# A two-layer graph network on one core: where the edge product is computed and added

## The chip, the cores and the metric

One NeuronCore of one Trainium2 chip runs the whole program in one launch. The metric is the device time of that launch in microseconds. Engines are named as in the profile: PE (TensorE) with its weight loads PEld, DVE (VectorE), ACT (ScalarE), POOL (GpSimd), and SP, which only issues transfers here.

## The reference, cut to what matters

There are 12,500 nodes with 128 features and 200,000 edges, sorted by their target node. Two layers follow each other. The second one needs, for every edge, the product of its 128 edge features with a 128x128 matrix.

```python
h = relu(layernorm(x))
x = x + gin(h)                     # neigh = segment_sum(h[src], dst); two dense layers after it
h = layernorm(relu(layernorm(x))) * gamma + beta
t = gelu(concat([h[src], edge_attr], axis=1) @ Wt + bt)
  # = gelu( (h @ Wt[:128] + bt)[src]  +  edge_attr @ Wt[128:] )
attn = sum((t @ Wk + bk) * (h[dst] @ Wq + bq), -1) * edge_weight / sqrt(128)
a = softmax of attn over the edges of one target node
out = x + gelu(segment_sum(a * (t @ Wv + bv), dst))
```

The line after `t` shows the split that both kernels use. The source part is computed once for each node and kept in memory as `source_rows` (L130). The edge part, `edge_attr @ Wt[128:]`, is here called the edge product.

## The kernel before, in words

**Chunks.** The edges are cut into 98 chunks of 2,048 (`CHUNK`, L39): 16 columns of 128 edges, one edge to a partition. Four columns are a quad, so a chunk has four quads. Both sweeps go over all chunks. A loop around each sweep repeats it when the targets of a block of 256 edges span over 40 nodes; with these inputs each sweep runs once.

**First sweep** (`gin_sweeps`, L510). For chunk c, SP loads the source indices and the transposed edge features (L548, L550). POOL gathers 16 columns of source rows with one indirect transfer each (L506, called at L561), after a small tensor operation that stands in front of each chunk (`hold`, L500). TensorE computes the edge product of chunk c, one matmul of 128 edges with `wt` for each column (L572), into two PSUM banks. ScalarE copies each quad from PSUM to `ews` (L602) and issues its store to the DRAM tensor `edge_products` (L610). Then TensorE takes up the gathered rows of chunk c-1 and sums them into windows of 40 nodes by a matmul with a one-hot matrix (L583). VectorE builds the one-hot matrix (L467) and adds the eight windows of a chunk to `acc` (L629).

**Between the sweeps** `node_mid` runs the dense layers of all nodes and writes `source_rows`.

**Second sweep** (`attention_sweeps`, L858). Each engine has a step that handles four chunks at different ages: f (the newest), mid (one older), late (two older) and last (three older). The order within a step is written out by hand for every engine.
- SP (L936 to L967), for f: indices, then four quads of stored edge products, each after VectorE's addition of the same quad of the chunk before (L944), then edge weights, the queries `qw` and their bias `cw`; then for last the broadcast `fade` (L960).
- POOL (L971): waits for the indices and until the sums of chunk c-4 have used its buffer (there are four `t` buffers, L974); then 16 gathers, in groups of four with a semaphore each.
- VectorE (L1220): `add_products` (L1118) waits for each gathered quad and its edge product and adds the one to the other in SBUF (L1123); then `add_sums` of last (L1163), the mask `misses` of f (L1127), the maxima of mid (L1183, eight at L1200, then L1203, L1205, L1216), and the scores of f (L1129 to L1161).
- ScalarE (L1099): gelu of a quad in place in SBUF (L1079), then the copy of the turned quad from PSUM to `tT` (L1084); at the end of the step the exponentials of mid (L1090, L1093).
- TensorE (L1051): it turns each gelu quad with four transposes (L988) into one of two PSUM banks, and multiplies the turned quad with the queries (L1003). Between these stand the transposes of mid's scores (L1012), the row of maxima (L1021) and the spread of the running maximum (L1027). The step ends with the sums of late (L1035 to L1049): 16 matmuls of a gelu tile with the exponentials (L1040) and 16 with ones (L1047).

A float32 matmul appears in the trace as two instructions, a transpose as one. `node_end` closes with the last projection and gelu.

Of the kernel before, what the change touches and what calls it, by code (L numbers as in the profile page):

```python
# [121 lines left out]
def build_gnn(nc, a):  # L122

    with ExitStack() as ctx:
# [9 lines left out]
        ew = nc.dram_tensor("edge_products", [NCH, P, COLS * D], F32, kind="Internal").ap()  # L134
# [21 lines left out]
        gin_sweeps(nc, a, g, h0, ew, first, span)  # L156
        node_mid(nc, a, g, res, arow, qk, ck)
        with nc.sbuf_tensor("rows", [33, NW], F32) as rows:
            g["rows"] = rows
            attention_sweeps(nc, a, g, arow, ew, qk, ck, fades, first, span)  # L160
            node_end(nc, a, g, res)
# [348 lines left out]
def gin_sweeps(nc, a, g, h0, ew, first, span):  # L510


    with ExitStack() as ctx:
        st = Stage(nc, ctx, "gin")
        wt = st.sb("wt_edge", [P, D])
# [3 lines left out]
        evT, ews = st.two("evT", [P, COLS * P]), st.two("ews", [P, COLS, D])  # L519
        sums = [st.ps(f"sums{j}") for j in range(2)]  # L520
        ew_ps = [st.ps(f"ew_ps{j}") for j in range(2)]
# [4 lines left out]
        ev_in, ew_out = st.sem2("ev_in"), st.sem2("ew_out")  # L526
        hot_ready, sums_ready, added = st.sem("hot_ready"), st.sem("sums_ready"), st.sem("added")
        product, ew_sb = st.sem("product"), st.sem("ew_sb")
        src = a["src_chunks"]
        dve_regs = [nc.vector.alloc_register(f"gin_win{b}") for b in range(BPC)]  # L530
        with nc.Block() as block:
            @block.sync
            def _(sp):
                sp.dma_start(wt[:, :], a["Wt"][D:2 * D, :]).then_inc(setup, 16)
                sp.dma_start(g["start"][:, :], first).then_inc(setup, 16)
                sp.wait_ge(setup, 32)
        with nc.Fori(0, span + 1, WIN):
            st.clear(gathers=True)
            next_windows(nc, g, st, w, hs[0][:, :, :].rearrange("p k d -> p (k d)"))
            with nc.Block() as block:  # L540
                @block.sync
                def _(sp):
                    def step(f, bk):
                        if not f:
# [20 lines left out]
                def _(pe):  # L565
                    def edge_product(f, q):
                        if q == 0:
                            wait(pe, ev_in[f.j], 16 * (f.h + 1))
                        wait(pe, ew_sb, QUADS * f.c + q - 1)
                        for k in range(4):  # L570
                            at = (4 * q + k) * P
                            mm = pe.matmul(ew_ps[q % 2][:, k * P:(k + 1) * P], evT[f.j][:, at:at + P],  # L572
                                           wt[:, :], start=True, stop=True)
                        mm.then_inc(product, 1)

# [11 lines left out]
                    def step(f, bk):  # L587
                        if f:
                            for q in range(QUADS):
                                edge_product(f, q)  # L590
                        if bk:
                            add_rows(bk)
                    over_chunks(pe, step)

                @block.scalar
                def _(act):
                    def step(f, bk):
                        def copy_product(q):
                            wait(act, product, QUADS * f.c + q + 1)
                            if q == 0:  # L600
                                wait(act, ew_out[f.j], 16 * f.h)
                            act.activation(ews[f.j][:, 4 * q:4 * q + 4, :].rearrange("p k d -> p (k d)"),  # L602
                                           ew_ps[q % 2][:, :], ACT.Copy).then_inc(ew_sb, 1)

                        if not f:
                            return
                        for q in range(QUADS):
                            copy_product(q)
                        wait(act, ew_sb, QUADS * (f.c + 1))
                        act.dma_start(ew[bass.ds(f.c, 1)].rearrange("a p n -> p (a n)"),  # L610
                                      ews[f.j][:, :, :].rearrange("p k d -> p (k d)")).then_inc(ew_out[f.j], 16)
                    over_chunks(act, step)
                    for j in range(2):
                        act.wait_ge(ew_out[j], 16 * (NCH // 2))
# [243 lines left out]
def attention_sweeps(nc, a, g, arow, ew, qk, ck, fades, first, span):  # L858
# [4 lines left out]
    with ExitStack() as ctx:  # L863
# [5 lines left out]
        ews = [st.sb(f"ews{q}", [P, COLS // QUADS, D]) for q in range(QUADS)]  # L869
# [20 lines left out]
        ew_in = [st.sem(f"ew_in_{q}") for q in range(QUADS)]  # L890
        wgt_in = st.sem2("wgt_in")
        names = ("summed", "t_sb", "tT_ps", "tT_sb", "sc_q", "miss", "biased", "prod", "score", "attn", "masked", "xm", "xm_ps",
# [10 lines left out]
        with nc.Block() as block:  # L903
            @block.sync
            def _(sp):
                sp.dma_start(g["start"][:, :], first).then_inc(setup, 16)

# [3 lines left out]
                sp.wait_ge(setup, 48)  # L911
# [18 lines left out]
        with nc.Fori(0, span + 1, WIN):  # L930
            st.clear(gathers=True)
            next_windows(nc, g, st, w, t[0][:, :, :].rearrange("p k d -> p (k d)"))
            with nc.Block() as block:
                @block.sync
                def _(sp):
                    def loads(f):  # L936
# [6 lines left out]
                        for q in range(QUADS):  # L943
# [170 lines left out]
                def _(v):  # L1114
# [266 lines left out]
```

## Time and profile before

| | |
|---|---|
| median of 3 runs | 4691.19 us (4682.67 to 4695.08) |
| profiled execution, its own time | 4713.18 us |
| its span in the trace | 4711.2 us |
| mean granted clock of TensorE | 0.729 |
| busy PE / DVE / ACT / POOL | 65% / 40% / 28% / 67% |
| first gather of the first sweep to the last one's end | 139 to 2128 us |
| first gather of the second sweep to the last one's end | 2443 to 4526 us |

The profile takes one execution. Its rows name an instruction group by line, engine and operation, then what it writes and reads, how many there were, the busy time, the mean of one in ns, and the idle time in front of it with the releaser that ended it.

### The profile page before, as it was taken

How to read it: one execution, taken by the hardware profiler on the slowest of the kernel's cores; microseconds unless marked ns; L12 is line 12 of the kernel's file. 1: busy time of each engine (PE TensorE's matmuls, PEld its weight loads, DVE VectorE, ACT ScalarE, POOL GpSimd, SP SyncE). 2: the span in 40 equal slices, each digit the busy share in tenths (PEclk: the TensorE clock that was granted, in tenths of full speed). 3: DMA queues.
4: the chain of work that ended last, by engine and by line, in shares of the span. 5: the costliest groups of instructions: out<-in, count | busy, mean ns of one | idle time of the engine just before them, and what ended most of it. 6: DMA issues, size and time to landing. Idle time of an engine off the chain costs nothing. (4 is left out here: it accounts for less than half of the span.)

```text
span 4711.2 us, 72968 instructions
## 1 busy us (share of the span) xinstructions
PE 3054.1 (65%) x20056; PEld 2809.9 (60%) x20057; DVE 1865.5 (40%) x5996; ACT 1313.3 (28%) x2114; POOL 3162.9 (67%) x3343
## 2 busy tenths in 40 slices
PE   2466666556665666664746777676767777777774
PEld 1466566556665666663326767676666666766664
DVE  3111111111111111114545666666666666666643
ACT  4111111111111111113633343343333343434324
POOL 0677777777777777770037777777777777777730
PEclk9666666666666666667877787788888787888776
DMA  4455445555455545542334444444444444444423
GB/s 123 150 159 159 148 152 159 159 159 157 144 158 159 159 144 156 159 141 64 102 101 115 125 122 117 113 127 121 118 124 116 124 116 123 117 126 118 121 61 101
DMA packets 364892, 614.69 MB, mean 130 GB/s; under 512 B 109604, under 2 KB 237335, under 8 KB 339624
## 3 DMA queue, kind: packets, MB, share of 16 engines
q1 hardware_dynamic: 237284, 298.04, 22.2%
q0 software_dynamic: 100352, 205.72, 16.9%
q10 hardware_dynamic: 27076, 109.29, 5.6%
q14 instruction: 160, 1.31, 0.1%
q8 instruction: 20, 0.33, 0.0%
HBM read 477.54 MB, written 135.23 MB: 130 GB/s over the span
## 5 line engine op out<-in xcount | busy, mean ns | idle before, releaser
L506 POOL DMA_INDIRECT attention_t<-source_rows,attention_idx x1568 | 1587.9, 1013 | 463.4 <-issue 447.7
L506 POOL DMA_INDIRECT gin_hs<-h_rows,gin_idx x1568 | 1506.7, 961 | 463.1 <-issue 463.0
L583 PE MATMUL gin_sums<-gin_hot,gin_hs 128*128 128x40 f32 x3136 | 686.6, 413 | 763.7 <-DMA gin_hs<-h_rows,gin_idx 763.7
L583 PEld LDWEIGHTS gin_sums<-gin_hot,gin_hs 128*128 128x128 f32 x3136 | 672.5, 330 | 781.8 <-issue 725.0
L629 DVE TENSOR_TENSOR acc<-acc,gin_sums 128x40 f32 x784 | 154.5, 197 | 1760.7 <-PE gin_sums L583 1670.3
L602 ACT ACTIVATE gin_ews<-gin_ew_ps 128x512 f32<-128x512 f32 x392 | 234.1, 597 | 1768.3 <-PE gin_ew_ps L572 1768.0
L988 PE MATMUL attention_tT_ps<-ident,attention_t 128*128 128x128 f32 x1568 | 366.5, 378 | 385.4 <-ACT attention_t L1079 385.4
L572 PE MATMUL gin_ew_ps<-gin_wt_edge,gin_evT 128*128 128x128 f32 x3136 | 566.2, 363 | 7.6 <-DMA gin_evT<-in_edge_attr_cols 7.6
L572 PEld LDWEIGHTS gin_ew_ps<-gin_wt_edge,gin_evT 128*128 128x128 f32 x3136 | 554.1, 277 | 8.9 <-DMA gin_evT<-in_edge_attr_cols 8.8
L988 PEld LDWEIGHTS attention_tT_ps<-ident,attention_t 128*128 128x128 f32 x1568 | 266.9, 199 | 421.8 <-issue 367.1
L1003 PE MATMUL attention_sc_q<-attention_qw,attention_tT 128*128 x3136 | 515.6, 325 | 1.2
L1003 PEld LDWEIGHTS attention_sc_q<-attention_qw,attention_tT 128*128 128x128 f32 x3136 | 504.3, 245 | 8.3 <-issue 4.2
L1079 ACT ACTIVATE attention_t<-attention_t 128x512 f32<-128x512 f32 x392 | 243.0, 627 | 548.6 <-DVE attention_t L1123 548.6
L1084 ACT ACTIVATE attention_tT<-attention_tT_ps 128x512 f32<-128x512 f32 x392 | 234.1, 597 | 550.6 <-PE attention_tT_ps L988 550.4
L1040 PE MATMUL attention_sum_ps<-attention_e_hot,attention_t 128*128 128x96 f32 x3136 | 375.3, 278 | 0.0
L1040 PEld LDWEIGHTS attention_sum_ps<-attention_e_hot,attention_t 128*128 128x128 f32 x3136 | 359.3, 192 | 12.3 <-issue 0.2
L1123 DVE TENSOR_TENSOR attention_t<-attention_t,attention_ews 128x512 f32<-128x512 f32 x392 | 251.1, 690 | 223.2 <-DMA attention_t<-source_rows,attention_idx 163.3
L1021 PE MATMUL attention_row_bank<-ident,attention_bm 80*1 80x80 f32 x784 | 97.5, 287 | 192.6 <-DVE attention_bm L1183 192.3
L1200 DVE TENSOR_TENSOR attention_mnew<-attention_mnew,attention_row_bank 1x40 f32 x784 | 144.3, 184 | 188.0 <-issue 61.6
L1216 DVE TENSOR_TENSOR attention_below<-attention_masked,attention_row_bank 128x80 f32<-128x80 f32 x784 | 126.7, 231 | 201.6 <-PE attention_row_bank L1027 196.9
L922 POOL MEMSET rows<- 1x12928 f32 x1 | 10.9, 10863 | 279.6 <-POOLq L640 279.6
L1021 PEld LDWEIGHTS attention_row_bank<-ident,attention_bm 80*1 80x1 f32 x784 | 67.7, 101 | 213.2 <-DVE attention_bm L1183 198.2
(137 smaller groups left out, 2958.2 us busy)
## 6 DMA issues: line engine op xcount, KB each, us to landing
gin_evT<-in_edge_attr_cols SPq DMA_DIRECT2D x98, 1024.0 KB, 6.6
edge_products<-gin_ews ACTq DMA_DIRECT2D x98, 1024.0 KB
attention_ews<-edge_products SPq DMA_DIRECT2D x392, 256.0 KB
gin_hs<-h_rows,gin_idx POOLq DMA_INDIRECT x1568
attention_t<-source_rows,attention_idx POOLq DMA_INDIRECT x1568
attention_qw<-qk_cols SPq DMA_DIRECT2D x98, 160.0 KB
attention_cw<-qk_bias_cols SPq DMA_DIRECT2D x98, 132.0 KB
attention_fade<-fades SPq DMA_DIRECT2D x98, 132.0 KB
```

The source lines that it names most:

```text
L506: gp.indirect_dma_start(out=out[:, k, :], out_offset=None, in_=rows[:, :], compute_op=op, in_offset=bass.IndirectOffsetOnAxis(ap=idx[:, k: ...
L572: mm = pe.matmul(ew_ps[q % 2][:, k * P:(k + 1) * P], evT[f.j][:, at:at + P], wt[:, :], start=True, stop=True)
L583: mm = pe.matmul(sums[j][:, b * WIN:(b + 1) * WIN], hs[bk.k][:, k, :], hot[j][:, k, :], start=(k % SUB == 0), stop=(k % SUB == SUB - 1))
L602: act.activation(ews[f.j][:, 4 * q:4 * q + 4, :].rearrange("p k d -> p (k d)"), ew_ps[q % 2][:, :], ACT.Copy).then_inc(ew_sb, 1)
L629: v.tensor_tensor(g["acc"][:, bass.ds(at, WIN)], g["acc"][:, bass.ds(at, WIN)], sums[bk.j][:, b * WIN:(b + 1) * WIN], ALU.add).then_inc(ad ...
L988: mm = pe.transpose(tT_ps[q % 2][:, k * P:(k + 1) * P], t[f.k][:, 4 * q + k, :], g["ident"][:, :])
L1003: mm = pe.matmul(sc_ps[:, o:o + WIDE], tT[q % 2][:, (n % 4) * P:(n % 4 + 1) * P], qw[j][:, bass.ds(off, WIDE)], start=True, stop=True)
L1021: mm = pe.matmul(row_bank[0:1, k * 2 * WIN:(k + 1) * 2 * WIN], bm[:, k:k + 1], g["ident"][0:2 * WIN, 0:2 * WIN], start=True, stop=True)
L1040: mm = pe.matmul(sum_ps[:, bass.ds(off, WIDE)], t[bk.k][:, k, :], e_hot[j][:, k, :], start=False, stop=True, skip_group_check=True)
L1079: act.activation(x, x, ACT.Gelu).then_inc(s["t_sb"], 1)
L1084: act.activation(tT[q % 2][:, :], tT_ps[q % 2][:, :], ACT.Copy).then_inc(s["tT_sb"], 1)
L1123: v.tensor_tensor(x, x, ews[q][:, :, :], ALU.add).then_inc(s["summed"], 1)
```

## The change

The first sweep no longer loads edge features, multiplies them, copies the result or stores it; the DRAM tensor `edge_products` is gone. In the second sweep SP loads the transposed edge features in two halves of a chunk (512 KB each). TensorE turns the raw gathered rows of a quad with four transposes into one PSUM bank and adds the edge product to them there by one matmul of 512 columns whose stationary operand is the weight. ScalarE takes gelu from that bank into `tT`, which the score matmuls read. TensorE turns `tT` back with four transposes into another bank, and ScalarE copies it over the gathered rows in `t`, which the sums read. VectorE's addition is gone. Two PSUM banks hold the turned quads as before, but now one for each direction. `fade_row` has one buffer in place of two.

```diff
 def gin_sweeps(...)  # SP
-                        wait(sp, product, QUADS * (c - 1))
-                        sp.dma_start(evT[j][:, :], a["edge_attr_cols"][bass.ds(c, 1)].rearrange(
-                            "a d e -> d (a e)")).then_inc(ev_in[j], 16)
...
                     def step(f, bk):
-                        if f:
-                            for q in range(QUADS):
-                                edge_product(f, q)
                         if bk:
                             add_rows(bk)
...
-                @block.scalar
-                def _(act):
...
 def attention_sweeps(...)
-        ews = [st.sb(f"ews{q}", [P, COLS // QUADS, D]) for q in range(QUADS)]
+        evT = [st.sb(f"evT{half}", [P, CHUNK // 2]) for half in range(2)]
+        w_edge = st.sb("w_edge", [P, D])
...
-        fade_row, fade = st.two("fade_row", [1, SPAN]), st.two("fade", [P, SPAN])
+        fade_row, fade = st.sb("fade_row", [1, SPAN]), st.two("fade", [P, SPAN])
-        tT_ps = [st.ps(f"tT_ps{k}") for k in range(2)]
+        pre_ps, t_ps = st.ps("pre_ps"), st.ps("t_ps")
...
-                        for q in range(QUADS):
-                            wait(sp, s["summed"], QUADS * (c - 1) + q + 1)
-                            sp.dma_start(ews[q][:, :, :].rearrange("p k d -> p (k d)"),
-                                         ew[bass.ds(c, 1), :, 4 * q * D:4 * (q + 1) * D].rearrange(
-                                             "a p n -> p (a n)")).then_inc(ew_in[q], 16)
+                        for half in range(2):
+                            wait(sp, s["pre_ps"], QUADS * (c - 1) + 2 * half + 2)
+                            sp.dma_start(evT[half][:, :],
+                                         a["edge_attr_cols"][bass.ds(c, 1), :, half * CHUNK // 2:(half + 1) * CHUNK // 2].rearrange(
+                                             "a d e -> d (a e)")).then_inc(ev_in[half], 16)
...
+                    def turn_rows(f, q):
+                        c, h, j = f.c, f.h, f.j
+                        wait(pe, gathered[f.k][q], 64 * (f.g + 1))
+                        wait(pe, s["tT_sb"], QUADS * c + q)
+                        for k in range(4):
+                            pe.matmul(pre_ps[:, k * P:(k + 1) * P], t[f.k][:, 4 * q + k, :], g["ident"][:, :], is_transpose=True,
+                                      start=(k == 0), stop=False, skip_group_check=True)
+                        if q % 2 == 0:
+                            wait(pe, ev_in[q // 2], 16 * (c + 1))
+                        pe.matmul(pre_ps[:, :], w_edge[:, :], evT[q // 2][:, 512 * (q % 2):512 * (q % 2 + 1)],
+                                  start=False, stop=True, skip_group_check=True).then_inc(s["pre_ps"], 1)
+
                     def turn_gelu(f, q):
-                        c, h, j = f.c, f.h, f.j
-                        wait(pe, s["t_sb"], QUADS * c + q + 1)
-                        wait(pe, s["tT_sb"], QUADS * c + q - 1)
+                        c = f.c
+                        wait(pe, s["tT_sb"], QUADS * c + q + 1)
+                        wait(pe, s["t_sb"], QUADS * c + q)
                         for k in range(4):
-                            mm = pe.transpose(tT_ps[q % 2][:, k * P:(k + 1) * P], t[f.k][:, 4 * q + k, :], g["ident"][:, :])
-                        mm.then_inc(s["tT_ps"], 1)
+                            mm = pe.transpose(t_ps[:, k * P:(k + 1) * P], tT[q % 2][:, k * P:(k + 1) * P], g["ident"][:, :])
+                        mm.then_inc(s["t_ps"], 1)
...
                         if f:
                             load_offsets(pe, pe_regs[f.k], g, f.c)
-                            turn_gelu(f, 0)
+                            turn_rows(f, 0)
                         if mid:
                             turn_scores(mid)
                         if f:
-                            turn_gelu(f, 1)
+                            turn_rows(f, 1)
+                            turn_gelu(f, 0)
                             scores(f, 0)
                         if mid:
                             spread_maxima(mid)
                         if f:
+                            turn_rows(f, 2)
+                            turn_gelu(f, 1)
+                            scores(f, 1)
+                            turn_rows(f, 3)
                             turn_gelu(f, 2)
-                            scores(f, 1)
+                            scores(f, 2)
                             turn_gelu(f, 3)
-                            scores(f, 2)
                             scores(f, 3)
...
                     def gelu(f, q):
-                        wait(act, s["summed"], QUADS * f.c + q + 1)
-                        x = t[f.k][:, 4 * q:4 * q + 4, :]
-                        act.activation(x, x, ACT.Gelu).then_inc(s["t_sb"], 1)
-
-                    def copy_tT(f, q):
-                        wait(act, s["tT_ps"], QUADS * f.c + q + 1)
+                        wait(act, s["pre_ps"], QUADS * f.c + q + 1)
+                        wait(act, s["t_ps"], QUADS * f.c + q - 1)
                         wait(act, s["sc_q"], QUADS * f.c + q - 1)
-                        act.activation(tT[q % 2][:, :], tT_ps[q % 2][:, :], ACT.Copy).then_inc(s["tT_sb"], 1)
+                        act.activation(tT[q % 2][:, :], pre_ps[:, :], ACT.Gelu).then_inc(s["tT_sb"], 1)
+
+                    def copy_t(f, q):
+                        wait(act, s["t_ps"], QUADS * f.c + q + 1)
+                        act.activation(t[f.k][:, 4 * q:4 * q + 4, :].rearrange("p k d -> p (k d)"), t_ps[:, :],
+                                       ACT.Copy).then_inc(s["t_sb"], 1)
...
                     def step(f, mid, late, last):
-                        if f:
-                            add_products(f)
                         if last:
                             add_sums(last)
```

## Rows read from the trace of the kernel before

**Rows 1.** The page, part 1: busy time of each engine over the span.

```profile
PE 3054.1 (65%) x20056; PEld 2809.9 (60%) x20057; DVE 1865.5 (40%) x5996; ACT 1313.3 (28%) x2114; POOL 3162.9 (67%) x3343
```

**Rows 2.** Part 5 of the page, the gathers; then POOL's waits, 2320 to 4640 us.

```profile
L506 POOL DMA_INDIRECT attention_t<-source_rows,attention_idx x1568 | 1587.9, 1013 | 463.4 <-issue 447.7
L506 POOL DMA_INDIRECT gin_hs<-h_rows,gin_idx x1568 | 1506.7, 961 | 463.1 <-issue 463.0
...
POOL attention_t L506 <- PE attention_sum_ps L1040: 7.0, 23, 0.3
```

**Rows 3.** POOL's timeline: start, duration, instruction, idle before; first sweep, then second.

```profile
2066.51 0.95 POOL L506 DMA_INDIRECT gin_hs<-h_rows,gin_idx  x1 [0.31 <-issue]
2067.48 0.18 POOL L500 TENSOR_TENSOR spare<-ones 1x1 f32<-1x1 f32 x1
...
3009.94 1.59 POOL L506 DMA_INDIRECT attention_t<-source_rows,attention_idx  x1 [0.30 <-issue]
```

**Rows 4.** Part 5 of the page: the edge products of the first sweep.

```profile
L572 PE MATMUL gin_ew_ps<-gin_wt_edge,gin_evT 128*128 128x128 f32 x3136 | 566.2, 363 | 7.6 <-DMA gin_evT<-in_edge_attr_cols 7.6
```

**Rows 5.** VectorE's groups by form with SBUF operands: 2400 to 4500 us, last row 139 to 2130.

```profile
L1123 DVE TENSOR_TENSOR attention_t<-attention_t,attention_ews 128x512 f32<-128x512 f32 x384 | 245.9, 690 | 217.5 <-DMA attention_t<-source_rows,attention_idx 157.7 <-issue 59.6
...
L1155 DVE SCALAR_TENSOR_TENSOR attention_masked<-attention_miss,attention_attn 128x640 f32<-128x640 f32 x95 | 79.6, 838 | 3.3
...
L1161 DVE TENSOR_TENSOR attention_xm<-attention_masked 128x320 f32<-128x320 f32 x95 | 46.7, 492 | 3.3
...
L1193 DVE TENSOR_TENSOR attention_mnew<-rows 1x264 f32 x95 | 39.1, 411 | 0.0
...
L467 DVE TENSOR_TENSOR gin_hot<-iota,rel 128x640 f32<-128x640 f32 x96 | 79.3, 826 | 10.8 <-issue 10.8
```

**Rows 6.** TensorE's timeline late in one step of the second sweep.

```profile
3025.49 0.64 PE L988 MATMUL attention_tT_ps<-ident,attention_t 128*128 128x128 f32 x4
3025.96 2.06 PE L1003 MATMUL attention_sc_q<-attention_qw,attention_tT 128*128 x16
3027.95 0.71 PE L1027 MATMUL attention_row_bank<-attention_mnew,ones 1*128 1x264 f32 x2
...
3028.94 3.81 PE L1040 MATMUL attention_sum_ps<-attention_e_hot,attention_t 128*128 128x96 f32 x32
3032.68 1.34 PE L1047 MATMUL attention_tot_ps<-attention_e_hot,ones 128*33 128x40 f32 x32
```

**Rows 7.** TensorE's timeline in `node_mid`: a 448-column matmul, and transposes.

```profile
2211.28 1.77 PE L729 MATMUL node_mid_pb<-node_mid_m_q,node_mid_w_WkT 128*128 128x448 f32 x4
...
2223.19 1.69 PE L751 MATMUL node_mid_pa<-ident,node_mid_m_hn 128*128 128x128 f32 x14
```

**Rows 8.** TensorE's timeline in the second sweep, after waits.

```profile
3012.64 1.11 PE L988 MATMUL attention_tT_ps<-ident,attention_t 128*128 128x128 f32 x4 [2.80 <-ACT attention_t L1079]
...
3021.77 1.23 PE L1021 MATMUL attention_row_bank<-ident,attention_bm 80*1 80x80 f32 x8 [4.66 <-DVE attention_bm L1183]
```

**Rows 9.** Busy time of PE, PEld, DVE, ACT, POOL in a stretch, granted clock, DMA.

```profile
2400.00:4500.00 2100.00, 1505.90 (x12112) 1367.00 (x12110) 1359.14 (x3996) 806.43 (x1153) 1617.05 (x1650) 0.80 0.43 119
...
3011.00:3012.00 1.00, 0.00 (x0) 0.00 (x0) 1.00 (x3) 0.12 (x1) 0.69 (x2) 0.95 0.00 0
...
3026.00:3027.00 1.00, 1.00 (x11) 0.94 (x9) 0.46 (x2) 0.82 (x2) 0.85 (x1) 1.00 0.29 66
```

**Rows 10.** Gelu in the second sweep, from part 5 of the page.

```profile
L1079 ACT ACTIVATE attention_t<-attention_t 128x512 f32<-128x512 f32 x392 | 243.0, 627 | 548.6 <-DVE attention_t L1123 548.6
```

**Rows 11.** SP's waits, 2500 to 4500 us; then its timeline.

```profile
SPq L945 <- DVE attention_t L1123: 1467.1, 148, 18.4
...
3022.19 0.33 SPq L942 DMA_DIRECT2D attention_idx<-in_src_chunks  x1
```

**Rows 12.** The last chunk: VectorE's last addition, then TensorE's spread.

```profile
4530.13 0.69 DVE L1123 TENSOR_TENSOR attention_t<-attention_t,attention_ews 128x512 f32<-128x512 f32 x1 [5.63 <-DMA attention_t<-source_rows,attention_idx]
...
4541.90 0.71 PE L1027 MATMUL attention_row_bank<-attention_mnew,ones 1*128 1x264 f32 x2
```

More of the change, by code:

```diff
@@ L155, in build_gnn @@
         span = nc.values_load(g["span"][0:1, 0:1], min_val=0, max_val=N)
-        gin_sweeps(nc, a, g, h0, ew, first, span)
+        gin_sweeps(nc, a, g, h0, first, span)
         node_mid(nc, a, g, res, arow, qk, ck)
@@ L159, in build_gnn @@
             g["rows"] = rows
-            attention_sweeps(nc, a, g, arow, ew, qk, ck, fades, first, span)
+            attention_sweeps(nc, a, g, arow, qk, ck, fades, first, span)
             node_end(nc, a, g, res)
@@ L565, in _ @@
                 def _(pe):
[L566 to L574, printed above, removed]
                     def add_rows(bk):
@@ L593, in _ @@
                     over_chunks(pe, step)
-                @block.scalar
-                def _(act):
[L597 to L606, printed above, removed]
-                        for q in range(QUADS):
[L608 to L614, printed above, removed]
                 @block.vector
@@ L855, in _, with attention_sweeps @@
             pairs(v, [residual, scales1, sources, renorm, scales2], [sources])
-def attention_sweeps(nc, a, g, arow, ew, qk, ck, fades, first, span):
+def attention_sweeps(nc, a, g, arow, qk, ck, fades, first, span):
     with ExitStack() as ctx:
@@ L889, in attention_sweeps @@
         gathered = [[st.sem(f"gathered_{k}_{q}") for q in range(QUADS)] for k in range(4)]
-        ew_in = [st.sem(f"ew_in_{q}") for q in range(QUADS)]
+        ev_in = st.sem2("ev_in")
         wgt_in = st.sem2("wgt_in")
-        names = ("summed", "t_sb", "tT_ps", "tT_sb", "sc_q", "miss", "biased", "prod", "score", "attn", "masked", "xm", "xm_ps",
+        names = ("pre_ps", "tT_sb", "t_ps", "t_sb", "sc_q", "miss", "biased", "prod", "score", "attn", "masked", "xm", "xm_ps",
                  "bm", "bm_ps", "mold", "raised", "mnew_ps", "mdiff", "kept", "fade", "below", "e_hot",
@@ L910, in _ @@
                 sp.dma_start(ck[:, NP:NW], acc[0:1, 0:NW - NP]).then_inc(setup, 16)
[L911 removed]
+                sp.wait_ge(setup, 64)
             @block.vector
@@ L997, in scores @@
                             wait(pe, s["biased"], BPC * c)
-                        wait(pe, s["tT_sb"], QUADS * c + q + 1)
                         for n in range(4 * q, 4 * q + 4):
@@ L1030, in sums @@
                         c, h, j = bk.c, bk.h, bk.j
+                        wait(pe, s["t_sb"], QUADS * (c + 1))
                         wait(pe, s["e_hot"], c + 1)
@@ L1088, in exps @@
                         wait(act, s["mdiff"], c + 1)
-                        wait(act, fade_out[j], 16 * h)
-                        act.activation(fade_row[j][:, :], mdiff[:, :], ACT.Exp).then_inc(s["fade"], 1)
+                        wait(act, fade_out[1 - j], 16 * (h + j))
+                        act.activation(fade_row[:, :], mdiff[:, :], ACT.Exp).then_inc(s["fade"], 1)
                         wait(act, s["below"], BPC * (c + 1))
@@ L1096, in exps @@
                         wait(act, s["sadded"], c - 1)
-                        act.dma_start(fades[j:j + 1, :], fade_row[j][:, :]).then_inc(fade_out[j], 16)
+                        act.dma_start(fades[j:j + 1, :], fade_row[:, :]).then_inc(fade_out[j], 16)
                     def step(f, mid, late, last):
@@ L1116, in _ @@
                     win3 = lambda x: x.rearrange("p (b n) -> p b n", n=WIN)
-                    def add_products(f):
-                        for q in range(QUADS):
-                            wait(v, ew_in[q], 16 * (f.c + 1))
-                            wait(v, gathered[f.k][q], 64 * (f.g + 1))
-                            x = t[f.k][:, 4 * q:4 * q + 4, :]
-                            v.tensor_tensor(x, x, ews[q][:, :, :], ALU.add).then_inc(s["summed"], 1)
                     def misses(f):
```

21 lines of the change are left out of this document (7 added, 14 removed).

## The prediction, as it was put on record

> **What bounds the kernel now.** I first read the busy shares [rows 1]: POOL leads with 67%, PE has 65%, and neither is full. So I went to what ends the waits. The reader is to see that the gathers of both sweeps have idle time in front of them that nothing releases ("issue"), about 0.30 us each, and that in the second sweep only 7.0 us are put down to TensorE [rows 2]. POOL never pauses: a quiet gather takes 0.945 us (the timeline shows 0.94 and 0.95), the next starts 1.25 us after it, and 16 of them with the small operation in front make 20.1 us for a chunk [rows 3]. Two sweeps of 98 chunks are 4073 of the 4711 us. In the first sweep the edge products take 566 us of TensorE, yet POOL doesn't wait for them [rows 2, 4]. Whatever is taken off TensorE, ScalarE and the queues there is beside POOL's row of gathers, and so costs nothing now.
>
> The second question is why the second sweep is slower. Its gathers have a mean of 1013 ns against 961 in the first [rows 2]; some take 1.59 us [rows 3]. Over the quiet 945 ns that is 1568 x 68 ns = 107 us in the second sweep and 25 us in the first. The second sweep's chunk is (1587.9 + 463.4 + about 30 for the small operation) / 98 = 21.2 us. The gather of 1.59 us ran while VectorE passed from its masked scores to the additions of the edge product; a gather has no other partner that differs so much between the sweeps. VectorE works 65% of the second sweep [rows 9].
>
> **The change, part by part.** The sum is made against the profiled execution, 4713.2 us; it lies 0.5% above the median of 4691.2, and I carry the difference in us over to the median.
>
> First sweep: 98 loads of 1 MB, 1568 matmuls (566 us of PE), 392 copies and 98 stores go. All of it is covered by POOL's 20.1 us for a chunk [rows 2, 3], and POOL's gathers stay. Saved on the path: 0. If DMA traffic slowed the issue of gathers, there would be something to gain, but the first sweep moves more bytes than the second and has the shorter gathers [rows 2]. Bounds: 0 to its whole excess, 25 us. I take 0, since VectorE's one-hot operation, which can account for that excess, stays [rows 5]. SP is moved past two waits fewer there.
>
> Second sweep, VectorE: 4 additions of 690 ns for a chunk go [rows 5], 2.8 us of an engine that isn't the bound. Their worth lies in what they do to the gathers. VectorE's work on SBUF operands alone is 246 us of additions, three groups of 640 columns at 79 us, L1161 with 47 and five groups of 264 columns at 40 us [rows 5]: 730 us for 107 us of excess, or 0.147 us for each. By that the additions cause 36 us. The first sweep gives the other end: 25 us of excess beside 79 us of such work [rows 5], 0.32 each, and 79 us for the additions; the low end is 0, if the excess only moves. I take 40, near the value of the stage itself, and 4 us more for the small operation in front of the chunks, which also grew. The largest possible value is all 107.
> The 1.59 us gather is 0.64 us over a quiet one, nearly one addition. The Trainium skill (SBUF — State Buffer, "SBUF: two separate sides") has VectorE and GpSimd locking one port pair, and the loser blocked for the whole instruction. By that rule 392 additions could each hold back a gather for 0.69 us, 270 us in all; the total excess of 107 us shows that most additions hold back nothing for their whole length.
>
> Second sweep, TensorE: this is the price. I add up one step at the full clock, from start to start [rows 6]: four quads turned 4 x 0.47, scores 16 instructions in 1.99, so 4.0 for the chunk; spread and the two clearing matmuls 0.99; sums 3.74 and totals 1.34. With the transposes of mid's scores (0.47, like a quad) and the row of maxima (1.23 at half clock [rows 8], so 0.6) it is 13.0 us. Added: 16 transposes at 1.69/14 = 0.12, which is 1.9; and four matmuls of 512 columns. The trace has 448 columns in two instructions, four of them in 1.70 [rows 7], so 0.85 each and 0.97 for 512: 3.9. The step becomes 18.8 us. The two turned directions now have one bank each, so hand-offs to ScalarE show: after the first quad the gelu of 0.63 us [rows 10] is covered only by 0.47 us of transposes, with the semaphores about 0.3 us open; at the fourth quad some 0.2 us. That makes 19.3 us, beside POOL's 20.8. Cost on the path: 0, with 1.5 us to spare. Without that cover each us over 21.2 costs 98 us.
> This holds at full clock only. The stretch has a mean of 0.80 of 2.4 GHz [rows 9]. It is 1.2 GHz after waits: in the example it fell 2 us into the idle time ahead of the step and the transposes took twice as long [rows 8, 9]; it is back at full at 3026 us [rows 6, 9]. The waits ahead were 2.80 us for gelu, behind the addition, and 4.66 us for the maxima, which VectorE reaches only after the addition of the last gathered quad [rows 8]. After the change VectorE no longer waits for gathers, so the second of them should go, and the first shrinks to what POOL leaves, 1.5 us. When TensorE is late it has no idle time, stays at 2.4 GHz and catches up; only when it is early it waits. So it should follow POOL. Buffers give it room: a gather needs the sums of four chunks before.
>
> ScalarE: the same 8 operations for a chunk, gelu now from PSUM: 0. SP: four loads of 256 KB become two of 512 KB, the same bytes. Behind the wait for the bank (after TensorE's second and fourth quad) stand weights, queries, bias and the next indices. Before, the same queue stood behind VectorE's last addition, 1467 us of waiting, and the indices still went out at 3022 [rows 11], 15 us ahead of use. TensorE's fourth product is some 2 us later than the addition: covered. One `fade_row` buffer instead of two: a 1 KB store a chunk ago, 0.
>
> The end: after the last addition VectorE still does 264-column sums, mask and maxima before TensorE can spread at 4541.9 [rows 12]. These no longer wait for the last quad. From 4530.1: turning 0.9 and product 1.9 at half clock, then two quads' turning and scores 5.6: 4538.5. That saves 3 us.
>
> The sum: -40 - 4 - 3 = -47 us, 4666 in the profiled execution and **4644 us** for the median. What is late next is still POOL, with 20.8 us for a chunk. A measurement of this kernel can tell about 0.3% (14 us) from no change.
>
> **The rivals.**
> *A larger gain* (0.10): the additions cause what the first sweep's ratio says, 79 us, with 8 for the small operation and the end. 4604 us. For it: the longest gather stands beside an addition. Against: it would leave hardly any excess to 480 us of the other such work.
> *No change* (0.13): the excess moves to VectorE's other operations, or TensorE's step comes out near 21.2 us and eats the gain. 4691 less 3, 4688 us.
> *TensorE becomes the bound* (0.19), slower. Its work of 18.8 us at a mean clock of 0.85 takes 22.0 us, 0.8 more than now, times 98 is 78, less 3: 4766 us. If the clock stayed at 0.80 it would be 23.5 us and 4913. It decides where the step passes 21.2 us, at a mean clock of about 0.9. For it: every step has at least four hand-offs to ScalarE and three to VectorE in program order, and the clock fell after 2 us of idleness [rows 9]. Against: those hand-offs have other work beneath them, and idleness needs TensorE to be early.
> The Trainium skill (TensorE: Matmul & The Clock Gate, "HAM oscillation") says that repeated waits between bursts put TensorE back to the lower clock, so that every burst starts slow. By that, each step's wait for POOL makes part of the next step slow. The rows agree for the kernel before (0.80); whether it lasts when the work nearly fills the step, no row shows.
>
> **How the numbers follow.** The forecast has 0.58: 4644, its own range 4625 to 4670. With the larger gain that is 0.68 faster, 0.13 the same, 0.19 slower. The low end of the range is the larger gain, 4600. The high end takes in no change and half of the slower rival, up to 4740; what lies beyond is its clock below 0.87, about 0.08, and below 4600 about 0.05.
>
> **What would show it.** Right: the first sweep's gathers stay at about 961 ns and its length within 5 us; the second sweep's mean falls from 1013 to about 985 ns; POOL has no waits for the sums; the granted clock of the second sweep rises above 0.9 with TensorE busy about 90%, and VectorE falls to 53% (1113 of 2100 us). Wrong: POOL waiting for the sums or for indices by more than 50 us, a step of TensorE of more than 21 us with a clock near 0.8, or waits of TensorE on `tT` or `t` that add up to over 2 us for a chunk. If the gathers' mean doesn't fall, my reading of the additions is wrong.

## The result, and the profile after

The kernel after has a median of 4648.99 us (4 runs, 4647.58 to 4655.26), the kernel before 4687.89 us (4 runs; the first three of them gave the 4691.19 that the forecast started from). The ratio is 0.9919, with a 95% interval of 0.9901 to 0.9936: 39 us faster. The forecast was 47 us faster and 4644 us. The profiled execution of after took 4650.0 us, close to its median; the one of before, 4713.2, was 25 us over its own, so the two traces lie 63 us apart, and 24 of these are that one execution's.

The page of the kernel after: the span, part 1, then the two groups of gathers and the product in part 5.

```profile
span 4648.2 us, 68347 instructions
...
PE 2787.4 (60%) x19272; PEld 2305.8 (50%) x19273; DVE 1624.6 (35%) x5604; ACT 1057.5 (23%) x1722; POOL 3109.2 (67%) x3343
...
L505 POOL DMA_INDIRECT attention_t<-source_rows,attention_idx x1568 | 1532.7, 977 | 463.0 <-issue 448.6
L505 POOL DMA_INDIRECT gin_hs<-h_rows,gin_idx x1568 | 1519.6, 969 | 463.0 <-issue 463.0
...
L950 PE MATMUL attention_pre_ps<-attention_evT,attention_w_edge 128*128 128x512 f32 x784 | 406.0, 600 | 0.0
```

Beside [rows 2] the reader is to see two movements. The second sweep's gathers fell from 1013 to 977 ns: 56 us. The first sweep's rose from 961 to 969 ns: 13 us back. Between these lies an unchanged "issue" of 0.30 us a gather, so POOL still sets the pace of both sweeps. The 13 us need care: the same first sweep has 961 ns in before, 958 in f1 and 954 in f3 below, so one execution's mean can move by 7 ns (11 us); the time of f3 settles it. From the small operation before the first gather to the last gather's end the first sweep went from 1989.5 to 2002.1 us and the second from 2083.4 to 2016.5. After the last gather 179.9 us are left where 185.2 were. The first sweep's 566 us of edge products are gone from TensorE [rows 4], and the first sweep got longer all the same.

Busy time in stretches of after: PE, PEld, DVE, ACT, POOL, the granted clock, DMA share and GB/s. They answer to [rows 9].

```profile
700.00:720.00 20.00, 7.04 (x32) 6.90 (x32) 2.32 (x10) 0.00 (x0) 15.27 (x18) 1.00 0.20 52
2400.00:4400.00 2000.00, 1752.38 (x14217) 1380.90 (x14217) 1106.10 (x3550) 774.20 (x1134) 1518.42 (x1614) 0.98 0.43 123
2500.00:4400.00 1900.00, 1705.55 (x13989) 1350.84 (x13990) 1072.48 (x3506) 753.05 (x1105) 1462.46 (x1569) 1.00 0.44 124
```

TensorE works 88% of the second sweep, at 0.98 of full clock instead of 0.80; VectorE fell from 65% to 55%.

One step of TensorE in the second sweep of after, and VectorE's and POOL's work beside it, from the timelines.

```profile
3012.66 0.71 PE L996 MATMUL attention_row_bank<-attention_mnew,ones 1*128 1x264 f32 x2
...
3018.84 0.65 PE L946 MATMUL attention_pre_ps<-ident,attention_t 128*128 128x128 f32 x4
3019.32 1.02 PE L950 MATMUL attention_pre_ps<-attention_evT,attention_w_edge 128*128 128x512 f32 x2
3020.30 0.64 PE L981 MATMUL attention_xm_bank<-ident,attention_xm 128*80 128x128 f32 x4
3022.45 0.66 PE L946 MATMUL attention_pre_ps<-ident,attention_t 128*128 128x128 f32 x4 [1.51 <-ACT attention_tT L1054]
...
3032.71 0.71 PE L996 MATMUL attention_row_bank<-attention_mnew,ones 1*128 1x264 f32 x2
```
```profile
3018.90 0.83 DVE L1123 SCALAR_TENSOR_TENSOR attention_masked<-attention_miss,attention_attn 128x640 f32<-128x640 f32 x1
3019.76 0.49 DVE L1129 TENSOR_TENSOR attention_xm<-attention_masked 128x320 f32<-128x320 f32 x1
```
```profile
3017.79 0.94 POOL L505 DMA_INDIRECT attention_t<-source_rows,attention_idx  x1 [0.30 <-issue]
3019.04 1.50 POOL L505 DMA_INDIRECT attention_t<-source_rows,attention_idx  x1 [0.30 <-issue]
3020.85 0.94 POOL L505 DMA_INDIRECT attention_t<-source_rows,attention_idx  x1 [0.30 <-issue]
```

From one spread of the maximum to the next this step has 20.05 us, of which 1.51 are a wait for gelu. POOL's chunk has (4468.27 - 2451.78) / 98 = 20.58 us. The long gather lies exactly beside VectorE's masked scores and the maximum behind them, now that there are no additions.

### The profile page after: what moved, and what is told of

Same layout as the page of the kernel before. It is cut to its first block and busy times, and to the rows that moved or that the text cites. A ratio compares the mean times of both kernels' runs of the same rounds, so it can differ in the third digit from the quotient of the medians.

```text
span 4648.2 us, 68347 instructions
## 1 busy us (share of the span) xinstructions
PE 2787.4 (60%) x19272; PEld 2305.8 (50%) x19273; DVE 1624.6 (35%) x5604; ACT 1057.5 (23%) x1722; POOL 3109.2 (67%) x3343
## 3 DMA queue, kind: packets, MB, share of 16 engines
q14 instruction: 136, 1.11, 0.1%
## 5 line engine op out<-in xcount | busy, mean ns | idle before, releaser
L972 PE MATMUL attention_sc_q<-attention_qw,attention_tT 128*128 x3136 | 406.3, 273 | 0.0
L950 PE MATMUL attention_pre_ps<-attention_evT,attention_w_edge 128*128 128x512 f32 x784 | 406.0, 600 | 0.0
L972 PEld LDWEIGHTS attention_sc_q<-attention_qw,attention_tT 128*128 128x128 f32 x3136 | 383.9, 193 | 0.0
L1054 ACT ACTIVATE attention_tT<-attention_pre_ps 128x512 f32<-128x512 f32 x392 | 234.0, 597 | 629.7 <-PE attention_pre_ps L950 628.6
L1010 PE MATMUL attention_sum_ps<-attention_e_hot,attention_t 128*128 128x96 f32 x3136 | 376.9, 279 | 0.0
L1010 PEld LDWEIGHTS attention_sum_ps<-attention_e_hot,attention_t 128*128 128x128 f32 x3136 | 360.7, 193 | 12.3 <-issue 0.2
L946 PE MATMUL attention_pre_ps<-ident,attention_t 128*128 128x128 f32 x1568 | 256.2, 286 | 183.7 <-ACT attention_tT L1054 128.1
L946 PEld LDWEIGHTS attention_pre_ps<-ident,attention_t 128*128 128x128 f32 x1568 | 167.1, 142 | 245.6 <-ACT attention_tT L1054 151.1
L958 PEld LDWEIGHTS attention_t_ps<-ident,attention_tT 128*128 128x128 f32 x1568 | 190.1, 142 | 166.9 <-issue 157.4
L1058 ACT ACTIVATE attention_t<-attention_t_ps 128x512 f32<-128x512 f32 x392 | 232.6, 593 | 81.4 <-PE attention_t_ps L958 81.4
L958 PE MATMUL attention_t_ps<-ident,attention_tT 128*128 128x128 f32 x1568 | 240.2, 276 | 0.0
L1108 DVE TENSOR_TENSOR attention_biased<-attention_sc_q,attention_cw 128x80 f32<-128x80 f32 x784 | 128.0, 233 | 103.3 <-issue 75.3
```

Of the source, the lines that this page charges most:

```text
L946: pe.matmul(pre_ps[:, k * P:(k + 1) * P], t[f.k][:, 4 * q + k, :], g["ident"][:, :], is_transpose=True, start=(k == 0), stop=False, skip_g ...
L950: pe.matmul(pre_ps[:, :], w_edge[:, :], evT[q // 2][:, 512 * (q % 2):512 * (q % 2 + 1)], start=False, stop=True, skip_group_check=True).th ...
L958: mm = pe.transpose(t_ps[:, k * P:(k + 1) * P], tT[q % 2][:, k * P:(k + 1) * P], g["ident"][:, :])
L972: mm = pe.matmul(sc_ps[:, o:o + WIDE], tT[q % 2][:, (n % 4) * P:(n % 4 + 1) * P], qw[j][:, bass.ds(off, WIDE)], start=True, stop=True)
L1010: mm = pe.matmul(sum_ps[:, bass.ds(off, WIDE)], t[bk.k][:, k, :], e_hot[j][:, k, :], start=False, stop=True, skip_group_check=True)
L1054: act.activation(tT[q % 2][:, :], pre_ps[:, :], ACT.Gelu).then_inc(s["tT_sb"], 1)
```

## The experiments

Three groups of four kernels ran, each on another chip. The groups e and g met chips on which the kernel before took 6459 and 6474 us; the group f met one where it took 4687.91 us, against 4687.89 beside the kernel after. So times of the group f are compared with before and with after, and those of e and g only with before in their own group.

What is different on the chips of e and g shows in the first sweep of g2, TensorE's timeline; compare it with the one uninterrupted row of 32 in 7.04 us above.

```profile
703.23 0.22 PE L563 MATMUL gin_sums<-gin_hot,gin_hs 128*128 128x40 f32 x1 [3.28 <-issue]
706.73 0.23 PE L563 MATMUL gin_sums<-gin_hot,gin_hs 128*128 128x40 f32 x1 [3.28 <-issue]
```

A matmul takes as long as elsewhere, but 3.3 us pass before the next, and the trace names no engine of this core or transfer that ends them. All engines but POOL's row of gathers have such pauses, VectorE up to 17 us at one place in most steps, and POOL then waits for the sums: 1270 us in g2, where after has 6.7. So these eight runs can't say what an edit does to the time where POOL sets the pace. The length of a single gather, and what VectorE did beside it, can still be read in them, and I use only that. The first sweep of after, in four of these runs, has means within 2 ns of each other (952 to 954 in e2, e3, g1 and g2). Why these chips pause is open.

**f1 and e1: the additions cut.** Kernel before, all waits and transfers kept.

```diff
-                            x = t[f.k][:, 4 * q:4 * q + 4, :]
-                            v.tensor_tensor(x, x, ews[q][:, :, :], ALU.add)
+                            x = t[f.k][:, 4 * q:4 * q + 4, 0:1]
+                            v.tensor_tensor(x, x, ews[q][:, :, 0:1], ALU.add)
```

> The kernel before with VectorE's four additions of a chunk cut to one element of each tile (nearly all of the edge product is left out of the sum; waits, transfers and the first sweep are as before). On a chip where the kernel before takes about 4690 us. Theory (the additions hold back the issue of gathers): the second sweep's gathers fall from 1013 ns to about 980 and the time by 40 to 65 us. Rival (what helped was less traffic or VectorE's freedom from waiting for gathers): gathers at 1000 ns or more, time within 15 us of before.

> The kernel before with VectorE's four additions of a chunk cut to one element of each tile (waits, transfers and first sweep as they are; nearly all of the edge product is left out of the sum). Theory (the additions hold back the issue of gathers): the second sweep's gathers fall from a mean of 1013 ns to about 980, and the time by 40 to 65 us against the kernel before, as far as the whole change or farther. Rival (what went with the change was the stored product's traffic and VectorE's waits at the end): gathers stay at 1000 ns or more and the time within 15 us of before.

f1 took 4660.68 us, ratio to before 0.9939 (0.9923 to 0.9956), 27 us faster. The gathers of both sweeps in f1, and those of the second in e1, from part 5 of their pages by form:

```profile
L506 POOL DMA_INDIRECT attention_t<-source_rows,attention_idx x1568 | 1556.4, 993 | 462.9 <-issue 448.9 <-PE attention_sum_ps L1040 8.5 <-DMA attention_idx<-in_src_chunks 5.5
L506 POOL DMA_INDIRECT gin_hs<-h_rows,gin_idx x1568 | 1502.2, 958 | 462.8 <-issue 462.8
```
```profile
L506 POOL DMA_INDIRECT attention_t<-source_rows,attention_idx x1568 | 1506.4, 961 | 495.4 <-issue 495.4
```

The second sweep's gathers went from 1013 to 993 ns, 31 us, beside 27 us in the time. The 1013 ns are those of before's one profiled execution, 25 us over its median, so the time is the safer figure. The additions do hold back gathers, but they are 20 of the 36 ns that the whole change took off. The rival (within 15 us) falls; my lower figure of 40 us was not reached. On the slow chips the kernel before (g4) has 994 ns and e1 961, 52 us apart, though e1's time (6709 us, ratio 1.0426, 1.0272 to 1.0579) is longer than that of before.

**f3 and e4: the first sweep of before put back**, the second of after kept; `edge_products` is computed and stored, and not used.

```diff
-def gin_sweeps(nc, a, g, h0, first, span):
+def gin_sweeps(nc, a, g, h0, ew, first, span):
...
```

> The kernel after with the first sweep of before: edge products computed, copied and stored, then not used. By my sum this work costs nothing: time within 15 us of after. If it shifts VectorE's one-hot operation against the gathers, as the traces suggest (969 ns after, 961 before), it is 5 to 15 us faster than after, with first-sweep gathers back at 961. If traffic matters it is over 15 us slower.

> The kernel after with the first sweep of before: edge products computed, copied and stored, and then not used. The step of my sum says this work costs nothing: time within 15 us of after. The trace of after has first-sweep gathers of 969 ns against 961 and a first sweep 12.6 us longer; if the edge product's work shifts VectorE's one-hot operation against the gathers, this kernel is 5 to 15 us faster than after and its first-sweep gathers are back at 961. If traffic on the queues mattered, it is slower than after by over 15 us.

f3 took 4630.34 us, ratio to before 0.9883 (0.9866 to 0.9899). With 566 us more of TensorE and 2 MB more traffic a chunk it is 19 us faster than after: my sum (no difference) missed, and the shift of the one-hot operation was expected to give 5 to 15.

```profile
L506 POOL DMA_INDIRECT gin_hs<-h_rows,gin_idx x1568 | 1495.3, 954 | 462.8 <-issue 462.8
```

Its first-sweep gathers have 954 ns against 969, or 24 us. So taking the work away is what lengthened the first sweep. The timelines say how. This is the one-hot operation of after with the gather beside it:

```profile
1007.79 0.83 DVE L466 TENSOR_TENSOR gin_hot<-iota,rel 128x640 f32<-128x640 f32 x1
```
```profile
1007.94 1.50 POOL L505 DMA_INDIRECT gin_hs<-h_rows,gin_idx  x1 [0.30 <-issue]
```

In after, VectorE starts this operation as soon as TensorE's sums are done, which follow the last gather of a chunk by a fixed time; so it meets a gather at the same place each chunk: 96 of 98 overlap it by over 0.3 us, with a mean excess of the gather of 0.38 us (37 us together). With the edge products between, its place drifts against the gathers: in before 91 overlap by over 0.3 us, with a mean excess of 0.22 us (21 together), in f3 85, with 0.12 (12 together). e4 on the slow chip took 6617 us against 6459 of before (1.0293, 1.0166 to 1.0419).

**f4: the same one-hot operation with one SBUF input.** Kernel after, first sweep only.

```diff
+        iota_ps = st.ps("iota_ps")
...
+                v.tensor_copy(iota_ps[:, 0:WIN], g["iota"][:, :])
...
-                            onehot_op(v, g, hot[f.j], f.c)
+                            onehot_op(v, g, hot[f.j], f.c, steps=iota_ps)
```

> The kernel after, but in the first sweep the row of numbers 0 to 39 that the one-hot operation compares with lies in PSUM, so that this operation has one SBUF input instead of two. Nothing else moves. If a second SBUF input is what holds gathers back, the first sweep's gathers fall from 969 ns to 946 to 952 and the time by 25 to 38 us against after. If any VectorE work beside them does, or the output written to SBUF, they stay above 960 and the time within 10 us.

It took 4618.37 us (4612.96 to 4623.18), ratio to before 0.985 (0.9834 to 0.9867): 31 us faster than after and the fastest kernel of this study.

```profile
L506 POOL DMA_INDIRECT attention_t<-source_rows,attention_idx x1568 | 1536.7, 980 | 463.0 <-issue 449.7 <-DMA attention_idx<-in_src_chunks 7.3 <-PE attention_sum_ps L1018 5.8
L506 POOL DMA_INDIRECT gin_hs<-h_rows,gin_idx x1568 | 1482.9, 946 | 462.9 <-issue 462.9
```
```profile
1032.74 0.82 DVE L467 TENSOR_TENSOR gin_hot<-gin_iota_ps,rel 128x640 f32<-128x640 f32 x1
```

The operation lasts 0.82 us as before and still overlaps gathers, but the first sweep's mean is 946 ns, that of a quiet gather. It isn't VectorE's work that delays a gather, nor its place, but its second SBUF input.

The other traces say the same once their gathers are sorted by what VectorE did beside them. Call a gather long if it took over 50 ns more than the quiet 945. In the second sweep of before 352 of the 885 gathers that overlapped an operation with two SBUF inputs were long; they hold all but 2 of its 106 us of excess. Of the 454 that overlapped only other VectorE work none was. In after it is 141 of 689, and none of 483. Such other work is the addition of sums from PSUM, here in the first sweep of after with a gather of ordinary length inside it:

```profile
1025.92 2.50 DVE L585 TENSOR_TENSOR acc<-acc,gin_sums 128x40 f32 x8 [17.31 <-PE gin_sums L563]
```
```profile
1026.04 0.94 POOL L505 DMA_INDIRECT gin_hs<-h_rows,gin_idx  x1 [0.30 <-issue]
```

The Trainium skill (SBUF — State Buffer, "SBUF: two separate sides") names an operation of VectorE with two SBUF inputs as one that locks a port pair shared with GpSimd, against a GpSimd operation that reads SBUF; f4 and this sorting agree, though no run shows the port itself or what a gather's issue reads. Its "fully blocks" fits single gathers (0.83 us of operation, 0.56 of excess, in the rows above), but the mean price is less: 28 of the 100 gathers that overlap this operation in after aren't long.

**f2, e2 and e3: spare operations of VectorE.** Kernel after with four operations with two SBUF inputs at the head of VectorE's step; e3 has sums over the row instead, with one input.

```diff
+                        if f:
+                            for q in range(QUADS):
+                                wait(v, dum, QUADS * f.c + q)
+                                v.tensor_tensor(spare_a[:, :], spare_a[:, :], spare_a[:, :], ALU.max).then_inc(dum, 1)
                         if last:
                             add_sums(last)
```

> The kernel after with four operations of VectorE of 128x512, all operands in SBUF, on a spare tile at the head of its step. Theory: the gathers' mean goes from 977 ns back to 1000 or more and the time is 35 to 60 us over after. Rival (the additions hurt through who waits for them): gathers within 5 ns of 977, time within 10 us of after.

> The kernel after with four VectorE operations of 128x512 for a chunk put at the head of VectorE's step, both inputs and the output in SBUF, on a spare tile that nothing else uses. Theory: they bring back the gathers' excess, mean from 977 ns to 1000 or more, time 35 to 60 us longer than after. Rival (the additions hurt by making others wait, not by their port): gathers stay within 5 ns of 977, time within 10 us of after.

> The same as the run before, but the four spare operations are sums over the row of 128x512: one input in SBUF, one column out, about as long. If what holds gathers back is a second SBUF input, the gathers stay at 977 ns (within 5) and the time within 10 us of after. If it is any busy VectorE, or its changed phase, they grow as in the run before.

f2 took 4838.08 us (1.0324, 1.0307 to 1.0341), 189 us more than after, and its gathers are shorter, 970 ns. Both theories missed. Its waits (2400 to 4500 us) and its TensorE show why:

```profile
POOL spare L499 <- PE attention_sum_ps L1013: 138.9, 65, 6.4
```
```profile
3005.37 1.22 PE L993 MATMUL attention_row_bank<-ident,attention_bm 80*1 80x80 f32 x8 [3.48 <-DVE attention_bm L1154]
3006.52 1.11 PE L949 MATMUL attention_pre_ps<-ident,attention_t 128*128 128x128 f32 x4
...
3023.05 2.86 DVE L1195 TENSOR_TENSOR attention_spare_a<-attention_spare_a 128x512 f32<-128x512 f32 x4
```

The 2.86 us stand before the reduction that gives the maxima; TensorE waits for it 3.48 us in its own order, the granted clock then reads 0.50 and the transposes take 1.11 us for four instead of 0.66, and the next spread is late, on which VectorE's next scores wait. The step became (4648.57 - 2452.79) / 98 = 22.4 us, over POOL's 20.6. This is the slower rival's mechanism, reached from the side of VectorE, and it says how near it was: 2.86 us more cost 1.8 a chunk. The spare operations did hold back gathers: those that overlap them have 29 of the second sweep's 39 us of excess, where the whole of after's was 51. What stands beside the scores fell by more (13 us beside the masked scores, where after has 26), and so the mean fell; that this goes with the longer steps is not tested. On the slow chip e2 and e3 took 6338.38 and 6338.23 us (0.986, 0.9742 to 0.9978, and 0.9868, 0.9751 to 0.9985), but their second-sweep gathers have 967 and 961 ns. Gather by gather the difference is sharp. Of those that overlap the spare operations and no masked scores or maximum (L1126, L1132), 119 of 211 are long in e2 (16 us of excess) and none of 215 in e3 (0.2 us). Each run has four spare operations a chunk, at the same place; only e2's have two SBUF inputs.

**g1, g2, g3, g4.** The product's matmul twice, the product cut to 32 columns, f4 with the attention values in PSUM as well, and the kernel before once more.

```diff
+                        for again in range(1):
+                            pe.matmul(pre_ps[:, :], w_edge[:, :], evT[q // 2][:, 512 * (q % 2):512 * (q % 2 + 1)],
+                                      start=False, stop=False, skip_group_check=True)
```
```diff
-                        pe.matmul(pre_ps[:, :], w_edge[:, :], evT[q // 2][:, 512 * (q % 2):512 * (q % 2 + 1)],
+                        pe.matmul(pre_ps[:, 0:32], w_edge[:, :], evT[q // 2][:, 512 * (q % 2):512 * (q % 2) + 32],
```
```diff
-        miss, attn = st.sb("miss", [P, COLS, WIN]), st.sb("attn", [P, COLS])
+        miss = st.sb("miss", [P, COLS, WIN])
...
+        attn = xm_bank[:, 0:COLS]
```

> The kernel after with the 512-column matmul of the edge product issued twice for each quad, so that the product is added twice: 4 x 0.96 us more of TensorE for a chunk. My sum gives TensorE's step 19.3 us beside POOL's 20.6. Theory (TensorE is just covered): the step becomes TensorE's own, 19.3 + 3.9 = 23.2 us, 2.6 over POOL's, 255 us more than after (4900), clock above 0.95, POOL waiting for the sums. Rival (TensorE's program still has idle time that takes the extra matmuls): under 100 us more.

> The kernel after with the product's matmul cut from 512 to 32 columns for each quad (so most of the edge product is left out): about 3.3 us less of TensorE for a chunk. Theory (POOL sets the pace): within 12 us of after, gathers at 977 ns within 6. Rival (TensorE's step is the bound, or near enough that hand-offs reach POOL): 20 us or more faster than after.

> The run with the row of numbers in PSUM, and in the second sweep the 16 attention values of a chunk in PSUM too, so that the masked-score operation has one SBUF input instead of two. In the trace of after, gathers that overlap this operation and the maximum behind it hold 25 of the second sweep's 48 us of excess. If the second SBUF input is what counts: gathers 980 ns down to 963 to 972, 10 to 26 us faster than 4618. If not: gathers within 3 ns of 980 and the time within 5 us of 4618.

> The kernel before, profiled a second time, since its first profile was 25 us over the median of its runs. If the excess of the second sweep's gathers is a property of the kernel, their mean is 1013 ns within 5. If it depends on how the engines' steps fall against each other in one execution, it is 990 to 1005 ns in an execution near 4690 us.

All four met the chip with the pauses: 6421, 6241, 6320 and 6516 us, beside 6474 of before (ratios 0.991, 0.9643 and 0.9763 for the first three). What TensorE's margin is was to come from g1 and g2 and didn't. In g3 the gathers have 945 and 954 ns; in g2, with both operations' inputs in SBUF, 952 and 960. That is 6 ns or 9 us in the second sweep for the attention values, in the direction expected but under the 8 to 17 ns that I gave. Beside the masked-score operation 38 of 139 gathers are long in g2 (13 us of excess) and none of 141 in g3 (1.5 us). That g3 beats f4 where POOL sets the pace isn't shown. g4's second-sweep gathers have 994 ns, which says nothing of an execution near 4690 us.

## Why the prediction was right, point by point

- **POOL bounds both sweeps: right.** 0.30 us of "issue" in front of every gather stayed, and POOL's waits for the sums came to 6.7 us against 7.0.
- **The first sweep's work was covered: right; that taking it away changes nothing: wrong.** "Saved on the path: 0", with bounds of 0 to 25 us of gain. It was a loss, outside these bounds: 12.6 us in the traces (I had said within 5), and f3 gives 19 us in the time. The step that failed is that the one-hot operation "stays": it did, but its place against the gathers moved.
- **Removing the additions shortens gathers: right; the term was mis-sized.** f3 has only the second sweep changed and is 58 us faster than before on the same chip; my terms for that sweep and the end were 40, 4 and 3, so 47. The additions alone (f1) are 27 of the 58, where I had 40. The other 30 lie between f1 and f3, and their traces say where: 21 us in gathers (993 against 979 ns), 5 in the small operation, 4 after the last gather. The same operations with two SBUF inputs (the product of scores and mask, the masked scores, the mask, the row of maxima) stand in both, but in f3 fewer gathers are long beside them, 143 against 245. I had no term for that. It fits the change of place that the first sweep showed; what moved them no run separates.
- **TensorE's price is covered: right, with less to spare than I said.** A 512-column product takes 0.86 us from its start to the next instruction's, 0.98 for the first of this step (forecast 0.97), and the step has 18.5 us of work (18.8). The hand-off after the first quad was put at 0.3 us and is 1.51 in this step, 1.38 on average. I had counted gelu's 0.63, but not the table load of 1.28 us, which in after stands behind the waits. These are the loads of before (groups by form, 2400 to 4500 us) and of after (part 5 of the page), with their idle time at the end:

```profile
L1079 ACT ACT_TABLE_LOAD x95 | 121.9, 1283 | 35.7 <-PEq L437 34.0
```
```profile
L1054 ACT ACT_TABLE_LOAD x97 | 124.5, 1283 | 487.5 <-PE attention_pre_ps L950 453.9
```

  Before, the load ran in idle time right behind the exponentials; now it starts when the first quad's product is done. With it this step of TensorE, which waits for no gather, takes 20.05 us against POOL's 20.58: 0.5 us to spare, where I had 1.5. What put the load behind the waits no run tests; in after gelu has three of them, in before one.
- **The clock rises by itself: right.** 0.98 in the second sweep, and 1.00 from 2500 us on. The durations agree: four transposes take 0.66 us, as in [rows 6] with 0.64, and from 2507 to 4400 us no wait of TensorE was over 1.7 us. So the slow bursts that the prediction took from the Trainium skill (TensorE: Matmul & The Clock Gate, "HAM oscillation") didn't come about in after; in f2, after a wait of 3.48 us, one did.
- **The end: right.** 3 us forecast, 5.3 measured after the last gather.

The forecast of 47 us against 39 came out near partly by luck: a gain of 58 us was taken as 47, and a loss of 19 us in the first sweep was left out.

## What to carry to other kernels

Where GpSimd issues gathers back to back, as here, their issue is the bound, and VectorE operations with two SBUF inputs beside it are part of the critical path, though VectorE is half idle. Putting the small operand in PSUM left the operation at 0.82 us, took one bank and removed the first sweep's whole excess (969 to 946 ns, 31 us in the time). Work taken off a covered engine can still lengthen the kernel, because it shifts what meets what. And when the waits in front of an activation change, look where the table load stands.

## What the runs showed of the hardware that I had not expected

- **A granted clock can be recorded wrong.** f2 and after have the same first sweep. The same stretch of f2 reads

```profile
700.00:720.00 20.00, 7.05 (x32) 6.90 (x32) 2.40 (x9) 0.00 (x0) 15.26 (x18) 0.50 0.20 52
```

  with 32 instructions in 7.05 us at "0.50", and after has 32 in 7.04 us at "1.00" (first section). The durations agree, so the two columns can't both be right. In the second sweep of after, at full clock, 32 instructions with 96 columns take 3.81 us (L1010, same weight size), and these 32 have 40 columns and take 7.04: it is the 1.00 that is wrong. After's first sweep ran at 1.2 GHz, and its mean clock of 0.973 over the span is too high; its other three executions, 4648 to 4655 us, are recorded with 0.752 or 0.753. Check the column against durations. The Trainium skill (TensorE: Matmul & The Clock Gate, "Seeing it yourself") warns that such records are unreliable on this chip; here they were.
- **The same program can be 38% slower on another chip** (6459 and 6474 against 4688 us), through pauses on the engines for which the trace shows no releaser on this core, while the gathers' own length is even lower (994 against 1013 ns for the kernel before).
